# Multi-query attention on one core: 32-row score tiles, the mask inside the maximum, and TensorE's other work as one piece per head between the second and third fill

## The chip, the cores and the metric

One Trainium2 chip, one of its cores. The metric is the device time of one execution in microseconds, as the median of several runs. TensorE multiplies matrices, VectorE, ScalarE and GpSimd (POOL) do elementwise work and reductions, SyncE (SP) issues the DMAs. SBUF is the on-chip memory of 128 partitions; PSUM, where TensorE writes, has eight banks of 128 x 512 f32. The engines run their own instruction queues in order and wait for each other by semaphores.

## The reference, cut to what matters

The whole computation is a multi-query attention, a transformer of six layers with local attention, and normalisations around both. The change touches the first alone (here with B, S = 8, 512):

```python
D_MODEL, NUM_HEADS, HEAD_DIM = 128, 16, 8
Q = (x @ Wq + bq).reshape(B, S, H, Dh).transpose(0, 2, 1, 3)
K = x @ Wk + bk                      # one set of keys for all 16 heads
V = x @ Wv + bv
A = jnp.einsum('bhqd,bkd->bhqk', Q, K)
causal = jnp.tril(jnp.ones((S, S), dtype=bool))
A = jnp.where(causal, A, -jnp.inf)
P = jax.nn.softmax(A / np.sqrt(Dh).astype(np.float32), axis=-1)
O = jnp.einsum('bhqk,bkd->bhqd', P, V)
return O.transpose(0, 2, 1, 3).reshape(B, S, H * Dh) @ Wo + bo
```

## The kernel before

`mqa_stage` runs the attention for 8 batches of 16 heads, 128 heads in a pipeline that `steps()` counts as n, with batch b = n // 16 and head h = n % 16. Each engine has its own loop over the same steps, and what it does in a step is written out by hand with `if h == ...`. Four heads are a group (`PER_GROUP`); `i` is the head's place in it.

Each head is scored twice. `scores` computes query-by-key scores, six heads ahead (`AHEAD`), only to find each query's largest score. They go into two PSUM banks, `score[0]` and `score[1]`, in fills: query tile 3 (512 keys), then tile 2 (384) together with tile 0 (128), then tile 1 (256), which two neighbouring heads share, so five fills a pair (`PAIR_FILLS`). Each fill waits until the maximum of the fill two before it is taken (`at_least(pe, s_max, fill - 1)`). VectorE's `maxima` reduces them. GpSimd's `negated_maxima` writes the negated maximum, split into two f32r parts, into two further columns of the queries. `turn_with_max` transposes these queries, and `scoresT` computes key-by-query scores with the maximum already subtracted, into three banks `scoreT[0..2]` (512, 384 + 128 and 256 columns), from which ScalarE's `exps` writes the probabilities. GpSimd's `causal` zeroes their upper triangles. `weighted_values` multiplies them with the values and a column of ones, in 128*32 tiles, one column tile a head of the group. After a transpose VectorE's `weighted` divides by the sums.

A head has 8 values a slot of 32 rows (`SLOTS`): high parts, low parts, the high parts again, and the maximum's two. Four heads lie under each other in the 128 rows of `qT0` and `qT1`. All matmuls of scores use all 128 rows, so the keys of head place i must be zero in the other 96: GpSimd's `spread_keys` makes four copies `kT[:, i, :]` of `k_flat`, each multiplied by a 0/1 column `own_rows`. The causal mask of the diagonal blocks is added by a further bf16 matmul of the identity and `mask_qk`, on top of each fill.

On TensorE, a step first issues `scoresT(n, k)` and `scores(n + AHEAD, k)` in turn for k = 0, 1, 2, and then what else is due: values and their transposes, the input's transposes and projection (`turn_xn`, `project`), keys and queries (`turn_keys`, `turn_queries`), and for the batch before `turn_attn`, `project_out` and `turn_y`. One bank, `near`, takes the results of most of them, another, `out_bank`, the last three; `take` waits until the bank's last user is done. ScalarE's loop does the three exponentials of a step and then the copies out of these banks. `hi_parts` and `lo_parts` (ScalarE, VectorE) split the projection. VectorE takes the maxima first, then `weighted`, `lo_parts` and the statistics of the normalisations; GpSimd normalises.

The rest of the kernel (`layers_stage`, `output_stage`) is untouched. Its line numbers occur in rows of the trace: L1256 to L1258 are projections with 512 columns, L1284 are scores in 64*32 tiles.

## Time and profile before

| | us |
|---|---|
| median of 3 runs (lowest, highest) | 3549.22 (3547.38, 3552.28) |
| the profiled execution | 3546.17 |
| its span in the trace | 3544.4 |

Busy time over the span: TensorE matmuls 3327.0 us (94%), VectorE 2958.5 (83%), ScalarE 2699.2 (76%), GpSimd 2594.4 (73%). The multi-query stage is about the first eighth of the span; the layers are the rest. The shares over the whole span therefore say little about this stage, and its own stretches have to be read. How a line of the groups is read: line of the kernel, engine, operation, output <- inputs, shapes, count, then busy time and mean ns of one, then idle time of the engine before them and who ended it. A line in order of time has its start, its duration, the engine, the line, the count that it merges, and in brackets the idle time before it with its releaser. Durations of matmuls include their way through the array, so their starts tell the pace better than their ends.

### The profile page before, as it was taken

The page shows a single profiled execution, that of the slowest core. Times are in us where ns is not written, and L with a number is a line of the kernel's source. Part 1 is how long each engine was busy: PE and PEld are TensorE (multiplying, and loading weights), DVE is VectorE, ACT ScalarE, POOL GpSimd, SP SyncE. Part 2 cuts the span into 40 slices and gives each one's busy share as a digit, 9 for nine tenths or more (in the row PEclk, how much of TensorE's full clock was granted, in tenths as well). Part 3 has the DMA queues.
Part 4 walks back from the last instruction along what each step waited for, and adds up shares of the span by engine and source line. Part 5 has one row for each costly group of instructions (what it writes and reads, how often), then busy time and mean ns, then how long its engine had stood idle before and what let it go on. Part 6 is the DMA issues. An engine that isn't in the chain of part 4 may idle for free. (4 is left out here: it accounts for less than half of the span.)

```text
span 3544.4 us, 158585 instructions
## 1 busy us (share of the span) xinstructions
PE 3327.0 (94%) x66425; PEld 2792.0 (79%) x66426; DVE 2958.5 (83%) x4037; ACT 2699.2 (76%) x4132; POOL 2594.4 (73%) x3334
## 2 busy tenths in 40 slices
PE   7999759999999999999999999999999999999995
PEld 5666547888788888788888888888888888888874
DVE  6666568888888888988888888889888889888874
ACT  4666547888788888788888788887788888888873
POOL 4676567777777777777777777777777777777772
PEclk9999879999999999999999999999999999999997
DMA  2000013222223222223222232222232222222222
GB/s 59 4 7 7 10 48 92 67 65 70 71 71 90 68 65 69 72 72 89 70 67 64 77 96 65 65 71 59 77 96 70 65 67 66 70 72 71 67 59 66
DMA packets 161748, 228.22 MB, mean 64 GB/s; under 512 B 42264, under 2 KB 60640, under 8 KB 161504
## 3 DMA queue, kind: packets, MB, share of 16 engines
q1 hardware_dynamic: 161632, 226.85, 23.8%
q8 instruction: 51, 0.84, 0.1%
q14 instruction: 65, 0.53, 0.0%
HBM read 21.00 MB, written 4.19 MB: 7 GB/s over the span
## 5 line engine op out<-in xcount | busy, mean ns | idle before, releaser
L1170 POOL TENSOR_TENSOR by_cos<-by_cos,by_sin 128x1024 f32<-128x1024 f32 x384 | 910.7, 2382 | 12.5 <-DVE by_sin L1524 12.5
L1176 POOL TENSOR_TENSOR by_cos<-by_cos,norms 128x1024 f32<-128x1024 f32 x384 | 733.8, 1911 | 13.0
L1522 DVE TENSOR_TENSOR by_cos<-proj,turns 128x1024 f32<-128x1024 f32 x384 | 470.0, 1224 | 177.9 <-ACT squares L1412 152.7
L1256 PE MATMUL proj<-qkv_hi,xs_hib 128*128 128x512 f32 x1152 | 512.5, 445 | 48.3 <-DVE by_sin L1524 39.3
L1524 DVE TENSOR_TENSOR by_sin<-proj,turns 128x1024 f32<-128x1024 f32 x384 | 466.1, 1214 | 0.0
L1528 DVE TENSOR_REDUCE sumsb<-squares 128x16 f32<-128x1024 f32 x384 | 464.4, 1209 | 1.5 <-DVE w_lo L1591 1.5
L1258 PE MATMUL proj<-qkv_hi,xs_lob 128*128 128x512 f32 x1152 | 458.1, 398 | 0.0
L1257 PE MATMUL proj<-qkv_lo,xs_hib 128*128 128x512 f32 x1152 | 457.9, 397 | 0.0
L1412 ACT ACTIVATE squares<-proj 128x1024 f32<-128x1024 f32 x384 | 392.6, 1022 | 82.7 <-PE proj L1258 81.9
L1265 PE MATMUL ring<-ident,by_cos 128*128 128x128 f32 x3072 | 385.4, 273 | 8.2 <-DVE xT L1625 4.9
L1392 ACT ACTIVATE vb<-proj 128x1024 f32<-128x1024 f32 x192 | 195.0, 1016 | 257.0 <-DMA v_win<-vb 225.5
L1265 PEld LDWEIGHTS ring<-ident,by_cos 128*128 128x128 f32 x3072 | 349.9, 141 | 35.2 <-issue 7.5
L1319 PE MATMUL ring<-attnT,wo 128*128 128x256 f32 x1536 | 347.2, 379 | 1.5 <-ACT attnT L1392 1.5
L1184 POOL TENSOR_TENSOR xs_lob<-xsb,xs_hib 128x128 fp32r<-128x128 f32 x192 | 88.3, 460 | 349.8 <-ACT xs_hib L1392 349.8
L1319 PEld LDWEIGHTS ring<-attnT,wo 128*128 128x128 f32 x1536 | 291.3, 190 | 44.8 <-ACT attnT L1392 2.0
L1256 PEld LDWEIGHTS proj<-qkv_hi,xs_hib 128*128 128x128 f32 x1152 | 219.0, 190 | 108.6 <-DVE by_sin L1524 61.0
L1305 PEld LDWEIGHTS ring<-v_win,pTb 64*32 64x32 f32 x24576 | 254.7, 105 | 56.4 <-issue 56.4
L1284 PEld LDWEIGHTS score<-kTb,qTb 64*32 64x32 f32 x24576 | 255.0, 105 | 54.4 <-issue 42.1
L1305 PE MATMUL ring<-v_win,pTb 64*32 64x64 f32 x24576 | 286.6, 226 | 7.5 <-issue 7.5
L1284 PE MATMUL score<-kTb,qTb 64*32 64x64 f32 x24576 | 286.5, 226 | 5.4 <-issue 4.8
L1392 ACT ACTIVATE kTb<-ring 128x1024 f32<-128x1024 f32 x192 | 197.7, 1030 | 101.5 <-PE ring L1265 101.0
L1258 PEld LDWEIGHTS proj<-qkv_hi,xs_lob 128*128 128x128 f32 x1152 | 218.6, 190 | 52.4
(196 smaller groups left out, 7985.6 us busy)
## 6 DMA issues: line engine op xcount, KB each, us to landing
v_win<-vb SPq DMA_DIRECT2D x1152, 128.0 KB, 2.3
v_win<-vb SPq DMA_DIRECT2D x768, 64.0 KB, 2.0
in_qkv<-L_ffn_Wqkv SPq DMA_DIRECT2D x12, 768.0 KB
wo<-L_ffn_Wo SPq DMA_DIRECT2D x6, 512.0 KB, 4.1
x_tok<-L_attn_x SPq DMA_DIRECT2D x8, 256.0 KB, 4.2
residual<-x_tok SPq DMA_DIRECT2D x8, 256.0 KB, 2.0
o_x<-residual SPq DMA_DIRECT2D x1, 2048.0 KB, 8.4
out<-o_x SPq DMA_DIRECT2D x8, 256.0 KB, 2.2
```

What stands on the lines that cost most here:

```text
L1170: nc.gpsimd.tensor_tensor(both, both, by_sin[:, j, :], ALU.add).then_inc(e[f"{w_}_added"].sem, 1)
L1176: nc.gpsimd.tensor_tensor(heads, heads, inverse, ALU.mult).then_inc(e[f"{w_}_ready"].sem, 1)
L1256: nc.tensor.matmul(out, xs_hi[:, tile], qkv_hi[:, cols], start=True, stop=False)
L1257: nc.tensor.matmul(out, xs_hi[:, tile], qkv_lo[:, cols], start=False, stop=False)
L1258: last = nc.tensor.matmul(out, xs_lo[:, tile], qkv_hi[:, cols], start=False, stop=True)
L1265: last = nc.tensor.transpose(out[:, i * P:(i + 1) * P], by_cos[:, t % 2, j, i * P:(i + 1) * P], ident[:, :])
L1284: last = nc.tensor.matmul(score[queries, at:at + KEYS], qT[rows, t % 2, i, queries], keys, start=False, stop=True, skip_group_check=True)
L1305: last = nc.tensor.matmul(out[queries, at:at + DH], pT[rows, i, queries], v_win[rows, t % 2, n, i, :], start=True, stop=True)
L1319: last = nc.tensor.matmul(out[:, 0:HS], wo[:, i, :], attnT[:, i, :], start=(i == 0), stop=(i == PAIRS - 1))
L1522: nc.vector.tensor_tensor(of_heads(by_cos[:, t % 2, j, :]), heads, table(0), ALU.mult)
L1524: nc.vector.tensor_tensor(swapped, heads, table(1), ALU.mult).then_inc(e[f"{w_}_rotated"].sem, 1)
L1528: nc.vector.tensor_reduce(sums[:, t % 2, j, :, 0], squares[:, :].rearrange("p (h d) -> p h d", d=DH), AX.X, ALU.add).then_inc(e[f"{w_}_sum ...
```

## The change

- `scores` and `scoresT` use the 32 rows of the head's own slot alone (`rows`), so `spread_keys`, `k_flat` and `own_rows` go; `kT` is one copy, which ScalarE writes out of `near`.
- The mask matmuls go. `maxima` is now one `tensor_tensor_reduce` each: scores plus an f32 mask row from SBUF, with the maximum as accumulator, its elementwise result into a scratch tile `masked`.
- Tile 1 has a fill of its own for each head: three fills a head (`FILLS`), six for a pair.
- All other TensorE work moves into `between(n, b, h)`, which stands between the second and the third fill of each step, with a new timetable; the values are split in two halves (i = 1 and 2). ScalarE has the same `between` ahead of its third exponential.
- VectorE takes the first two maxima of a step, then statistics, then the third, then `weighted` and `lo_parts`. Output normalisation and y come later by several heads, the input's normalisation earlier by one batch.
- The pipeline runs six steps longer.

```diff
-PAIR_FILLS = 5
+FILLS = 3
+QUERIES_AT = (8, 11, 12, 15)
+SUM_STATISTICS_AT = (6, 8, 9, 10)
-FIRST_STEP, LAST_STEP = -MQA_H, HEADS + 2 * MQA_H
+FIRST_STEP, LAST_STEP = -MQA_H, HEADS + 2 * MQA_H + 6
...
-    first = PAIR_FILLS * (m // 2)
-    return ((3, first), (2, first + 1), (1, first + 2)) if m % 2 == 0 else ((3, first + 3), (2, first + 4))
+    return (3, FILLS * m), (2, FILLS * m + 1), (1, FILLS * m + 2)
...
-        k_flat, own_rows = sb("a_k_flat", [P, S]), sb("a_own_rows", [P, PER_GROUP])
-        kT = [sb(f"a_kT{p}", [P, PER_GROUP, S], F32R) for p in range(2)]
+        kT = [sb(f"a_kT{p}", [P, S], F32R) for p in range(2)]
...
             def scores(m, qt, fill):
+                rows = slice(SLOTS * i, SLOTS * i + SLOTS)
                 out, keys = score[fill % 2], kT[b % 2]
                 at_least(pe, s_max, fill - 1)
-                queries = lambda k: qT0[:, g, k * P:(k + 1) * P]
+                queries = lambda k: qT0[rows, g, k * P:(k + 1) * P]
                 if qt == 3:
-                    if i % 2 == 0:
+                    if i == 0:
                         pe.wait_ge(q_done, GROUPS * b + g + 1)
-                        pe.wait_ge(keys_done, PER_GROUP * b + i + 2)
-                    nc.tensor.matmul(out[:, :], queries(3), keys[:, i, :], start=True, stop=True,
-                                     skip_group_check=True)
-                    masked, mask = out[:, 3 * P:4 * P], mask_qk[:, 0, :]
+                        pe.wait_ge(keys_done, b + 1)
+                    last = nc.tensor.matmul(out[:, :], queries(3), keys[rows, :], start=True, stop=True)
...
-                nc.tensor.matmul(masked, ident_bf[:, :], mask, start=False, stop=True,
-                                 skip_group_check=True).then_inc(s_full, 1)
+                    last = nc.tensor.matmul(out[:, 0:2 * P], queries(1), keys[rows, 0:2 * P], start=True, stop=True)
+                last.then_inc(s_full, 1)
...
+                    last = nc.tensor.matmul(scoreT[k][:, at:at + width], kT[b % 2][rows, kt * P:(kt + 1) * P],
+                                            qT1[rows, g, kt * P:S], start=True, stop=True)
...
+            def between(n, b, h):
+
+                group, i = n // PER_GROUP - 1, h % PER_GROUP
+                new, old, oldest = b + 1, b - 1, b - 3
+                if 0 <= group < B * GROUPS:
+                    if i in (1, 2):
+                        weighted_values(group, (0, 1) if i == 1 else (2, 3))
+                    elif i == 3:
+                        turn_values(group)
+                if i == 2 and 0 <= group + 2 < B * GROUPS:
+                    turn_with_max(group + 2)
+                if batch_of(new):
+                    if h == 0:
+                        turn_xn(new)
+                    elif h in (3, 4):
+                        project(new, h - 3)
+                    elif h == 7:
+                        turn_keys(new)
+                    elif h in QUERIES_AT:
+                        turn_queries(new, QUERIES_AT.index(h))
+                if batch_of(old):
+                    if h == 8:
+                        turn_attn(old)
+                    elif h == 12:
+                        project_out(old)
+                if batch_of(oldest) and h == 4:
+                    turn_y(oldest)
...
                 for k in range(3):
+                    if k == 2:
+                        between(n, b, h)
                     if 0 <= n < HEADS:
                         scoresT(n, k)
                     if k < len(ahead):
                         scores(n + AHEAD, *ahead[k])
...
             def maxima(m, qt, fill):
                 dve.wait_ge(s_full, fill + 1)
+                at_least(dve, s_max, fill - FILLS + 1)
+
+                def largest(qt, at):
+                    n = (qt + 1) * P
+                    place = slice((fill % FILLS) * S + at, (fill % FILLS) * S + at + n)
+                    return nc.vector.tensor_tensor_reduce(
+                        out=masked[:, place], in0=score[fill % 2][:, at:at + n], in1=mask_qk[:, 4 * P - n:4 * P], scale=1.0,
+                        scalar=LOWEST, op0=ALU.add, op1=ALU.max, accum_out=row_max[:, qt, h:h + 1])
...
-                for fill in fills(n + AHEAD):
+                new, old, older = b + 1, b - 1, b - 2
+                ahead = fills(n + AHEAD)
+                for fill in ahead[0:2]:
+                    maxima(n + AHEAD, *fill)
...
+                for fill in ahead[2:]:
                     maxima(n + AHEAD, *fill)
                 group = n // PER_GROUP - 1
                 if h % PER_GROUP == 3 and 0 <= group < B * GROUPS:
                     weighted(group)
-                if batch_of(new) and h in (4, 5):
-                    lo_parts(new, h - 4)
+                if batch_of(new) and h in (3, 4):
+                    lo_parts(new, h - 3)
```

## Rows read from the trace of the kernel before

**Rows 1.** One line of the kernel, the exponentials: durations, first and last start.
```profile
L545 ACT ACTIVATE a_probs<-a_scoreT x384: 383/594/674, 39.5 to 415.8; 128x512 f32<-128x512 f32 x128, 128x256 f32<-128x256 f32 x64
```

**Rows 2.** Busy time by stretch: length, busy (instructions) by engine, clock, DMA.
```profile
200.00:300.00 100.00, 94.63 (x773) 67.91 (x771) 67.49 (x176) 68.18 (x154) 70.10 (x129) 1.00 0.02 7
```

**Rows 3.** In order of time: the stage's last copy.
```profile
436.67 0.60 ACT L537 ACTIVATE xT<-a_out_bank 128x512 f32<-128x512 f32 x1 [6.94 <-PE a_out_bank L370]
```

**Rows 4.** In order of time, TensorE matmuls: an even and an odd head.
```profile
225.28 0.47 PE L411 MATMUL a_scoreT<-a_qT,a_kT 128*128 128x512 f32 x1
225.59 0.39 PE L383 MATMUL a_score<-a_kT,a_qT 128*128 128x512 f32 x1
225.82 0.23 PE L399 MATMUL a_score<-a_mask_qk,ident_bf 128*128 128x128 bf16 x1
...
227.30 0.60 PE L370 MATMUL a_near<-ident,a_qa 128*128 128x128 f32 x4
227.74 0.60 PE L370 MATMUL a_values<-ident,a_pvb 128*128 128x128 f32 x4
228.09 0.48 PE L411 MATMUL a_scoreT<-a_qT,a_kT 128*128 128x512 f32 x1
...
229.77 0.39 PE L383 MATMUL a_score<-a_kT,a_qT 128*128 128x512 f32 x1
```

**Rows 5.** The same view: values, the output projection, half an input projection.
```profile
208.45 0.48 PE L480 MATMUL a_out_bank<-a_bias,a_ones_r 128*128 128x512 f32 x1
...
209.57 0.48 PE L411 MATMUL a_scoreT<-a_qT,a_kT 128*128 128x512 f32 x1
...
233.60 2.36 PE L422 MATMUL a_values<-a_probs,a_va 128*32 128x512 f32 x32
235.89 0.50 PE L411 MATMUL a_scoreT<-a_qT,a_kT 128*128 128x512 f32 x1
...
243.72 0.38 PE L452 MATMUL a_near<-a_bias,a_ones_r 128*128 128x288 f32 x1
...
244.33 0.49 PE L411 MATMUL a_scoreT<-a_qT,a_kT 128*128 128x512 f32 x1
```

**Rows 6.** The same view in the layers: full tiles, then 64*32 tiles.
```profile
1522.09 0.40 PE L1258 MATMUL proj<-qkv_hi,xs_lob 128*128 128x512 f32 x1
1522.42 1.48 PE L1284 MATMUL score<-kTb,qTb 64*32 64x64 f32 x128
```

**Rows 7.** In order of time, TensorE and VectorE: maxima between fills.
```profile
36.89 0.28 PE L399 MATMUL a_score<-a_mask_qk,ident_bf 128*128 128x256 bf16 x1
...
37.21 0.56 DVE L742 TENSOR_REDUCE a_row_max<-a_score 128x1 f32<-128x384 f32 x1
...
37.68 0.28 DVE L743 TENSOR_REDUCE a_row_max<-a_score 128x1 f32<-128x128 f32 x1
37.88 0.68 DVE L745 TENSOR_REDUCE a_row_max<-a_score 128x2 f32<-128x512 f32 x1
...
38.02 0.50 PE L383 MATMUL a_score<-a_kT,a_qT 128*128 128x512 f32 x1
```

**Rows 8.** Groups by line and shape, the first 600 us: keys, a two-operand addition.
```profile
L281 POOL TENSOR_SCALAR a_kT<-a_k_flat,a_own_rows 128x512 fp32r<-128x512 f32 x32 | 49.6, 1562 | 2.1 <-ACT a_k_flat L537 2.1
...
L1522 DVE TENSOR_TENSOR by_cos<-proj,turns 128x1024 f32<-128x1024 f32 x19 | 23.3, 1224 | 33.4 <-ACT squares L1412 26.2 <-PE ring L1265 7.0
```

**Rows 9.** In order of time, VectorE: half of the low parts, `weighted`.
```profile
17.02 0.42 DVE L731 TENSOR_TENSOR a_qa<-a_near,a_qa 128x256 fp32r<-128x256 f32 x1 [2.40 <-ACT a_va L537]
...
205.80 0.25 DVE L752 RECIPROCAL a_recipb<-a_values 128x16 f32<-128x16 f32 x1
...
206.19 0.29 DVE L757 TENSOR_TENSOR a_attnb<-a_values,a_recipb 128x128 f32<-128x128 f32 x1
```

**Rows 10.** The same view at the start: first fill, first maximum.
```profile
22.80 0.77 PE L383 MATMUL a_score<-a_kT,a_qT 128*128 128x512 f32 x1 [0.33 <-POOL a_kT L281]
...
27.86 0.68 DVE L740 TENSOR_REDUCE a_row_max<-a_score 128x1 f32<-128x512 f32 x1
```

More of the change, by code:

```diff
@@ L166, in mqa_stage @@
         no_max = sem("no_max")
[L167 removed]
+        k_full, keys_done = sem("k_full"), sem("keys")
         q_full, q_done = sem("q_full"), sem("q")
@@ L309, in _ @@
                     negated_maxima((n + AHEAD) // PER_GROUP)
-                new, old, older = b + 1, b - 1, b - 2
+                next_, new, older = b + 2, b + 1, b - 2
                 if n == FIRST_STEP:
@@ L399, in scores @@
-                nc.tensor.matmul(masked, ident_bf[:, :], mask, start=False, stop=True,
-                                 skip_group_check=True).then_inc(s_full, 1)
+                    nc.tensor.matmul(out[:, 0:3 * P], queries(2), keys[rows, 0:3 * P], start=True, stop=True)
+                    last = nc.tensor.matmul(out[:, 3 * P:4 * P], queries(0), keys[rows, 0:P], start=True, stop=True)
+                else:
+                    last = nc.tensor.matmul(out[:, 0:2 * P], queries(1), keys[rows, 0:2 * P], start=True, stop=True)
@@ L407, in scoresT, with weighted_values @@
                     pe.wait_ge(t2_done, GROUPS * b + g + 1)
-                at = 0
+                at, rows = 0, slice(SLOTS * i, SLOTS * i + SLOTS)
                 for kt in PROB_BANKS[k]:
                     width = S - kt * P
-                    last = nc.tensor.matmul(scoreT[k][:, at:at + width], kT[b % 2][:, i, kt * P:(kt + 1) * P],
-                                            qT1[:, g, kt * P:S], start=True, stop=True)
+                    last = nc.tensor.matmul(scoreT[k][:, at:at + width], kT[b % 2][rows, kt * P:(kt + 1) * P],
+                                            qT1[rows, g, kt * P:S], start=True, stop=True)
                     at += width
                 last.then_inc(st_full, 1)
-            def weighted_values(group):
-                pe.wait_ge(causal_done, PER_GROUP * (group + 1))
-                at_least(pe, attn_done, group)
-                for kt in range(TILES):
+            def weighted_values(group, tiles):
+                if 0 in tiles:
+                    pe.wait_ge(causal_done, PER_GROUP * (group + 1))
+                    at_least(pe, attn_done, group)
+                for kt in tiles:
                     for i in range(PER_GROUP):
@@ L424, in weighted_values @@
                                                 start=(kt == 0), stop=(kt == TILES - 1))
-                last.then_inc(pv_full, 1)
+                if TILES - 1 in tiles:
+                    last.then_inc(pv_full, 1)
             def turn_values(group):
@@ L460, in turn_keys @@
                 pe.wait_ge(lo_done, 2 * b + 2)
-                take("near", (k_flat_done, b + 1))
+                take("near", (keys_done, b + 1))
                 turned(near, [ka[:, t, :, :].bitcast(F32).rearrange("p r s -> p (r s)") for t in range(TILES)], k_full)
@@ L603, in _, with between @@
             nc.scalar.activation(c["exp_warm"][:, :], c["minus_half"][:, 0:1], ACT.Exp)
[L604 to L606 removed]
+            def between(n, b, h):
                 group = n // PER_GROUP - 1
[L608 to L612 removed]
+                new, old, oldest = b + 1, b - 1, b - 3
+                if h % PER_GROUP == 2:
+                    if 0 <= group < B * GROUPS:
+                        values_group(group)
+                    if 0 <= group + 2 < B * GROUPS:
+                        turned_with_max(group + 2)
                 if batch_of(new):
[L614 removed]
+                    if h == 0:
                         turned_input(new)
[L616 to L617 removed]
+                    elif h in (3, 4):
+                        hi_parts(new, h - 3)
                     elif h == 7:
                         keys_turned(new)
[L620 to L623 removed]
+                    elif h in QUERIES_AT:
+                        queries_turned(new, QUERIES_AT.index(h))
                 if batch_of(old):
[L625 removed]
+                    if h == 8:
                         attn_turned(old)
[L627 removed]
+                    elif h == 12:
                         output(old)
[L629 to L630 removed]
+                if batch_of(oldest) and h == 4:
+                    output_turned(oldest)
+            for n, b, h in steps():
+                for k in range(3):
+                    if k == 2:
+                        between(n, b, h)
+                    if 0 <= n < HEADS:
+                        exps(n, k)
         @block.vector
```

188 lines of the change are left out of this document (55 added, 133 removed).

## The prediction

> **What bounds the kernel now.** I read the views from the outside in. First the span of the exponentials and the busy time by stretch [rows 1, 2]: the multi-query stage starts its exponentials, three a head for 128 heads, between 39.5 and 415.8 us; the last start is the last head's third, so 376.3 us hold about 127.6 heads, 2.95 us each, and the stage's last copy ends at 437.3 [rows 3]. The diff touches nothing behind that, so the question is what 2.95 us becomes. In 200 to 300 us TensorE is busy 95% of the time; VectorE, ScalarE and GpSimd stand at 67 to 70%, about 2.0 us a head. The granted clock there is 1.00, the 2.4 GHz level. So TensorE sets the pace, and I went on to its order of time in one pair of heads [rows 4].
>
> In rows 4 an even head's scores and transposed scores run from 225.28 to 227.30 = 2.02 us. The odd one starts at 228.09; the next head's first fill starts at 229.77 and lies 0.31 behind the transposed scores before it (as 225.59 does behind 225.28), so the odd head took 229.46 - 228.09 = 1.37. The mean is 1.70 us. The reader is to see that starts follow each other by columns: 512 columns take 0.23 (225.59 to 225.82).
>
> The rest of TensorE's work is the "pieces" [rows 5]. Two groups of four transposes take 228.09 - 227.30 = 0.79, so 0.40 a group. The weighted values of a group of four heads take 235.89 - 233.60 = 2.29, the output projection 209.57 - 208.45 = 1.12, half of an input projection 244.33 - 243.72 = 0.61. Per four heads come one set of values and three transposes; per batch of 16 heads four more transposes (input, keys, attention, y), two halves and one output projection. Per head: 2.29/4 + 3 x 0.40/4 + (4 x 0.40 + 2 x 0.61 + 1.12)/16 = 0.57 + 0.30 + 0.25 = 1.12. 1.70 + 1.12 = 2.82 of the 2.95; the rest is waits for maxima.
>
> **Part by part: what TensorE loses and gains.** The two and a half mask matmuls of a head go, and the shared fill of two heads becomes one fill of 256 columns a head. Scores and transposed scores then are 1280 columns each, 2560 x 0.23/512 = 1.15 us; I add 0.10 for the two 128-column matmuls, which are short beside their weight loads: 1.25 against 1.70. That is 0.45 us a head saved if nothing else changes.
>
> Against it stands the change of tile shape. Every one of the 16 pieces now stands between 32-row matmuls, so each head enters another shape and comes back. The trace of before has no 32-row tile. The nearest rows are the layers' 64*32 tiles [rows 6]: the 512-column matmul in front starts at 1522.09, and the tiled ones at 1522.42, 0.33 instead of 0.23. I take 0.10 for each change of shape, both ways, with bounds 0 and 0.20: 0.20 a head. The values split in two pay two more, 0.20 per four heads, 0.05 a head. The trace so bears out that a change costs something. The Trainium skill ("TensorEngine Tiling (Array Packing)", Key Properties) states it as a rule against this change: changing the tiling mode drains the engine, while another tile of the same mode does not. It gives no price.
>
> TensorE's own work then is 1.25 + 1.12 + 0.05 + 0.20 = 2.62 us a head, if matmuls of different row groups don't overlap.
>
> **The reductions on VectorE.** Four reductions a head instead of three and a half, over the same 1280 elements. Spacing [rows 7]: 37.21 to 37.68 for 384 elements is 0.47, 37.68 to 37.88 for 128 is 0.20, so 1.05 ns an element and 0.065 fixed. 1280 elements in four instructions are 1.35 + 0.26 = 1.61 us. The new instruction adds the mask from SBUF. A two-operand one with PSUM and SBUF inputs takes 1224 ns for 1024 elements [rows 8], about the same slope plus start, so the adding is free. What the accumulator's write-out costs no row shows: bounds are 0 and 0.20 each (a 128-element instruction). I take 0.07, the fixed part of one more instruction, since it moves a single column. That is 1.87 a head. Weighted values cost 205.80 to 206.48 = 0.68 per four heads [rows 9], and the statistics and low parts lift the sum to about 2.3, under TensorE's. The Trainium skill ("VectorE: DVE Perf Modes", Two Vector instructions with no wait between them) says that an operation that also writes out its accumulator is two instructions; no row here shows it.
>
> **The wait that the change adds.** There are two score banks and three fills a head, so fill k waits for the maximum of fill k-2. With the piece between the second and the third fill, the second fill of a head waits for the third maximum of the head before, which waits for the third fill, which stands in TensorE's queue behind the whole piece. TensorE's first fill and two transposed scores can run beside it, the piece can't. From the start of a second fill to the next:
> - its 512 columns 0.23, change of shape 0.10, the piece, change back 0.10
> - transposed scores of 256 columns ahead of the third fill: 0.12 alone, 0 if side by side; I take 0.06
> - the third fill, 256 columns, lasts 0.28, then 0.04 until VectorE starts (36.89 + 0.28 = 37.17, start 37.21) [rows 7]
> - maximum of 256 elements: 0.28 + 128 x 1.05 ns = 0.41, and 0.07 for the accumulator
> - back to TensorE 0.06 (37.68 + 0.28 = 37.96, the next fill starts at 38.02).
>
> Sum without the piece 1.35 us. The mean piece is 1.12 + 0.05 = 1.17, so 2.52.
>
> Some heads take longer, because VectorE's `weighted` comes after the third maximum and the next two maxima behind it. After it VectorE needs 0.68 + (0.60 + 0.47 + 0.20) + 3 x 0.07 = 2.16 until it can take a third maximum again; that fill is there after 0.87 + piece. The pieces at heads 0, 4, 8 and 12 are 0.40, 1.01, 0.80 and 1.52, so VectorE is late by 0.9, 0.3, 0.5 and 0. At head 4 another wait decides: `project` of the second half needs `lo_done` of the first, which VectorE makes after `weighted`, 0.68 + at least 0.42 [rows 9] after the third maximum; TensorE is there 0.39 after it. About 0.8 us, and behind it in TensorE's queue stand the y transposes, the transposed scores and the third fill. Together 0.9 + 0.8 + 0.5 = 2.2 us per batch, 0.14 a head. The two bounds (TensorE's 2.62, the ring of waits 2.52 + 0.14) lie side by side; I take 2.70, which leaves 0.04 for their meeting.
>
> **Off the path.** Spreading the keys goes from GpSimd, 32 instructions of 1562 ns, 0.39 us a head [rows 8]; GpSimd stands at 70%, so it buys nothing in the steady part. At the start TensorE's first fill waited 0.33 us for the spread keys and began at 22.80, but the first maximum began only at 27.86 [rows 10], behind the statistics in VectorE's queue; I take nothing. ScalarE has the same exponentials and copies, one key copy for one. Its copies now stand ahead of the third exponential, at most two of 0.60 us [rows 3], with 2.70 - 2.0 = 0.7 us of slack a head. No DMA moves except that the residual stores of a batch start later; the last one's chain (projection, two normalisations, y) is the same instructions in the same order, so the 21 us behind the last exponential stay. If ScalarE's cover is gone, it costs up to 0.6 us on one head in four, 0.15 a head.
>
> **Sum.** Heads with scores still ahead are 122 of 128. (2.95 - 2.70) x 122 = 30.5 us. The profiled run took 3546.17 (span 3544.4, 1.8 around it); 3546.2 - 30.5 = 3515.7. The median of the runs is 3.1 above the profiled one, so 3519.
>
> **Bounds.** Everything at its low end (no cost of shape, no accumulator, transposed scores side by side): 2.70 - 0.20 - 0.05 - 0.07 - 0.06 = 2.32, 77 us, 3472. Everything at its high end (0.20 for each change, 0.20 for the accumulator, 0.12 for the transposed scores): 2.70 + 0.20 + 0.05 + 0.13 + 0.06 = 3.14, 23 us slower, 3572.
>
> **Rivals.**
> 1. Row groups run side by side, and switching is nearly free: 2.35 to 2.55 a head, bound by VectorE (2.3) and the piece; 3475 to 3500. For it: 128 instructions of 64 columns in 64*32 tiles last 1.48 us [rows 6], 12 ns each, where 64 columns at 2.4 GHz alone are 27 ns, so tiles do overlap; but those tiles differ in columns too. The heads n and n+6 lie two row groups apart. Against it: the ring of waits has only one such pair in it. The Trainium skill ("TensorE: Matmul & The Clock Gate", Part 3) says that a single 32-row matmul takes as long as a full one and that the gain is concurrency, measured at 3.07 times for four tiles.
> 2. The ring eats the gain: shape changes near 0.20 each, 2.87 to 3.05 a head; 3540 to 3561. For it: a set of values in 128*32 tiles is entered and left by such changes too. Against it: the 0.10 of rows 6.
> 3. Slower, by VectorE: the fused reduction costs more than a plain one. VectorE's sum is 1.61 + 0.42 + 4a; it passes 2.95 when a, the surcharge of one instruction, passes 0.23 us. At 0.35, or two cycles an element (+1.33 a head), VectorE needs 3.4: 122 x 0.45 = 55 us, 3604. Against it: the two-operand row of rows 8.
> 4. Slower, by the clock: with a quarter of the rows at work and a wait a head, the granted clock falls to the 1.2 GHz level in part of the stage. TensorE's 2.62 doubles; for half of the stage that is 2.3 x 61 = 140 us, 3660. Against it: 1.00 in rows 2, and the longest new wait in the sum is 0.8 us.
>
> **How the numbers follow.** Forecast (3500 to 3535) 0.47; rival 1 0.18; rival 2 0.20; rival 3 0.10; rival 4 0.03; 0.02 for a stall in start or end. The range 3478 to 3566 leaves out rivals 3 and 4 and the ends of the bounds. A measurement tells 0.2%, 7 us, which is 0.06 us a head. Faster by more: 0.47 + 0.18 + 0.03 of rival 2 = 0.68; within: 0.09 of rival 2 and 0.01 = 0.10; slower: 0.08 + 0.10 + 0.03 + 0.01 = 0.22.
>
> **What would show it.** In the profile after: the exponentials' last start near 385 us; a second fill that starts 0.06 behind the third maximum of the head before; starts around a piece 0.10 wider than columns; 256-element reductions about 0.41 long, with or without a second instruction; a TensorE idle of 0.8 us before `project` at head 4. VectorE busy above 90% would make rival 3 right; a granted clock under 1.00 in 100 to 300 us rival 4. The prediction is wrong where the ring isn't what TensorE waits for, or the new instruction's price is far from 0.07.

## The result and the profile after

The kernel after takes 3588.85 us (median of 7 runs, 3566.93 to 3592.98) against 3549.22 (3547.38 to 3555.35): the ratio is 1.0099, 95% interval 1.0076 to 1.0121, so 1% slower. The prediction was 3519, faster. The profiled execution took 3592.98, its span 3591.0.

The first view is the exponentials' line, as in [rows 1] (durations, first and last start), and the busy time by stretch, as in [rows 2]: length, busy (instructions) for TensorE, its weight loads, VectorE, ScalarE, GpSimd, then the granted clock, the DMA share and GB/s.

```profile
L528 ACT ACTIVATE a_probs<-a_scoreT x384: 377/597/672, 42.5 to 463.6; 128x512 f32<-128x512 f32 x128, 128x256 f32<-128x256 f32 x64
```

```profile
100.00:200.00 100.00, 94.06 (x604) 57.69 (x605) 59.08 (x273) 57.67 (x133) 41.48 (x94) 0.74 0.01 4
200.00:300.00 100.00, 92.12 (x658) 56.58 (x660) 65.98 (x308) 61.94 (x142) 56.84 (x116) 0.85 0.02 7
300.00:400.00 100.00, 92.55 (x652) 58.39 (x640) 64.85 (x306) 61.76 (x143) 52.28 (x110) 0.82 0.02 6
```

The exponentials hold 421.1 us instead of 376.3, 44.8 more; the span grew by 46.6. All of the loss is in the attention. A head takes 421.1/127.6 = 3.30 us. TensorE's busy share is that of before (92 to 94% against 94.63), but the granted clock is 0.74 to 0.85 where [rows 2] had 1.00. With two levels, 2.4 and 1.2 GHz, a mean clock c means that 2(1 - c) of the stretch ran at the lower: 52, 30 and 36 us, 118 of these 300.

The clock column reads 1.00 ahead of the first change on record, which comes at 77.1 us. The matmuls show that the clock was low up to there. TensorE in order of time, one head of the start and two heads later on (a start, a duration, the tile and shape; in brackets the idle time before it):

```profile
65.58 0.57 PE L379 MATMUL a_score<-a_kT,a_qT 32*128 32x256 f32 x1
65.59 0.79 PE L391 MATMUL a_scoreT<-a_qT,a_kT 32*128 32x512 f32 x1
65.59 0.79 PE L374 MATMUL a_score<-a_kT,a_qT 32*128 32x512 f32 x1
...
66.72 0.68 PE L376 MATMUL a_score<-a_kT,a_qT 32*128 32x384 f32 x1
...
70.47 0.68 PE L376 MATMUL a_score<-a_kT,a_qT 32*128 32x384 f32 x1
```

```profile
246.62 0.38 PE L391 MATMUL a_scoreT<-a_qT,a_kT 32*128 32x256 f32 x1
...
246.62 0.38 PE L379 MATMUL a_score<-a_kT,a_qT 32*128 32x256 f32 x1
...
246.63 0.49 PE L391 MATMUL a_scoreT<-a_qT,a_kT 32*128 32x512 f32 x1
...
246.63 0.50 PE L374 MATMUL a_score<-a_kT,a_qT 32*128 32x512 f32 x1
...
247.56 0.44 PE L376 MATMUL a_score<-a_kT,a_qT 32*128 32x384 f32 x1 [0.20 <-DVE a_row_max L727]
...
247.84 0.22 PE L377 MATMUL a_score<-a_kT,a_qT 32*128 32x128 f32 x1
...
247.99 0.66 PE L360 MATMUL a_values<-ident,a_pvb 128*128 128x128 f32 x4
...
248.48 0.60 PE L360 MATMUL a_near<-ident,a_qa 128*128 128x128 f32 x4
...
249.01 0.38 PE L379 MATMUL a_score<-a_kT,a_qT 32*128 32x256 f32 x1
...
249.46 0.42 DVE L727 CUSTOM_DVE_ANT_0 a_masked<-a_score,a_mask_qk 128x256 f32<-128x256 f32 x1 [0.38 <-PE a_score L379]
...
249.81 0.08 DVE L727 DVE_READ_ACCUMULATOR2_ANT a_row_max<- 128x1 f32 x1
...
249.95 0.44 PE L376 MATMUL a_score<-a_kT,a_qT 32*128 32x384 f32 x1 [0.20 <-DVE a_row_max L727]
```

A matmul of 512 columns lasts 0.79 us in the first block and 0.50 in the second: the first is at 1.2 GHz, the second at 2.4. A head at the start takes 3.75 us (66.72 to 70.47), the same kind of head later 2.39 (247.56 to 249.95). Between the first and the last exponential 203 of the 421 us are at the half clock, 34.6 of them before 77.1, the rest mostly in stretches of 17 to 27 us, about one a batch (118.1 to 142.0 is the first).

What does that cost? The kernel rows128 below, the same but for the rows of the scores, takes 2.66 us a head with no lowered clock. Against it the heads of the kernel after that run at the full clock take 0.09 more (the same places in the batch, from the exponentials' starts), so a head at the full clock is about 2.75, and 127.6 of them are 350 us. That leaves 71 of the 421 us for the clock, 0.35 us lost for each us at the half clock. Two batches of 16 heads inside the kernel after agree: the fourth takes 48.2 us with 6.8 at the half clock, the fifth 54.4 with 23.9, a difference of 6.2 us for 17.1. The span of the exponentials is 421.1 - 127.6 x 2.70 = 77 us over the prediction: 71 of these are the clock's.

### The profile page after: what moved, and what is told of

It is laid out like the page before. It is cut to its first block and busy times, and to the rows that moved or that the text cites. A ratio compares the mean times of both kernels' runs of the same rounds, so it can differ in the third digit from the quotient of the medians.

```text
span 3591.0 us, 158808 instructions
## 1 busy us (share of the span) xinstructions
PE 3366.3 (94%) x66105; PEld 2775.8 (77%) x66106; DVE 2965.7 (83%) x4608; ACT 2691.8 (75%) x4132; POOL 2549.4 (71%) x3302
## 5 line engine op out<-in xcount | busy, mean ns | idle before, releaser
L1256 PEld LDWEIGHTS ring<-ident,by_cos 128*128 128x128 f32 x3072 | 350.2, 141 | 34.6 <-issue 7.5
L727 DVE CUSTOM_DVE_ANT_0 a_masked<-a_score,a_mask_qk 128x512 f32<-128x512 f32 (+3 forms) x512 | 229.5, 487 | 143.4 <-PE a_score L379 130.9
```

Of the source, the lines that this page charges most:

```text
L1256: last = nc.tensor.transpose(out[:, i * P:(i + 1) * P], by_cos[:, t % 2, j, i * P:(i + 1) * P], ident[:, :])
```

## The experiments

Every kernel is timed against the kernel before; the medians of that lay between 3544.52 and 3549.45 us. "Half clock, 100 to 400" is the sum of 2(1 - c) over three stretches of 100 us, which a reader can repeat from the windows; the next column is the whole time between first and last exponential, with the start by the durations of matmuls; "last" is the last exponential's start.

| kernel | rows of scores | median us | ratio (95%) | last | half clock, 100 to 400 | half clock, all |
|---|---|---|---|---|---|---|
| before | 128 | 3549.22 | 1 | 415.8 | 0 | 3 |
| after | 32 | 3588.85 | 1.0099 (1.0076, 1.0121) | 463.6 | 118 | 203 |
| rows128 | 128 | 3516.12 | 0.9915 (0.9898, 0.9931) | 379.7 | 0 | 0 |
| rows64 | 64 | 3544.52 | 0.9995 (0.9985, 1.0005) | 404.2 | 16 | 35 |
| fill128 | 32, and filler on 128 | 3582.88 | 1.0109 (1.0092, 1.0125) | 452.8 | 40 | 79 |
| fill32 | 32, and filler on 32 | 3606.35 | 1.0170 (1.0153, 1.0187) | 474.9 | 92 | 154 |
| late_pieces | 32 | 3622.11 | 1.0208 (1.0191, 1.0225) | 502.5 | 126 | 256 |
| thin128 | 128, few columns | 3513.18 | 0.9908 (0.9889, 0.9928) | 372.7 | 0 | 3 |
| before_fused | 128 | 3559.49 | 1.0038 (1.0024, 1.0052) | 424.1 | 0 | 7 |
| rows128_attn7 | 128 | 3514.32 | 0.9911 (0.9894, 0.9927) | 375.9 | 0 | 0 |
| before_rows32 | 32 for most | 3612.96 | 1.0178 (1.0161, 1.0195) | 478.9 | 78 | 124 |
| scores32 | 32 and 128 | 3665.28 | 1.0353 (1.0317, 1.0389) | 521.1 | 52 | 97 |
| after_attn7 | 32 | 3563.45 | 1.0029 (1.0015, 1.0044) | 442.6 | 88 | 165 |

(The 3, 3 and 7 us of before, thin128 and before_fused lie ahead of 58 us; from there to the last exponential the clock of the kernels with all scores on 128 rows is 1.00. What lies behind the last exponential isn't counted, so the windows of rows128, thin128 and rows128_attn7, which end at 373 to 380 us, give more than the table.) The times themselves are medians of 2 to 10 runs; the clock columns are of the one profiled run.

**rows128: is it the rows?** The kernel after with scores on all 128 rows and the keys spread by GpSimd as before; timetable, fills and fused maxima stay.

```diff
-                out, keys = score[fill % 2], kT[b % 2]
+                out, keys = score[fill % 2], kT[b % 2][:, i, :]
...
-                queries = lambda k: qT0[rows, g, k * P:(k + 1) * P]
+                queries = lambda k: qT0[:, g, k * P:(k + 1) * P]
...
-                    last = nc.tensor.matmul(out[:, :], queries(3), keys[rows, :], start=True, stop=True)
+                    last = nc.tensor.matmul(out[:, :], queries(3), keys[:, :], start=True, stop=True)
...
-                    last = nc.tensor.matmul(scoreT[k][:, at:at + width], kT[b % 2][rows, kt * P:(kt + 1) * P],
-                                            qT1[rows, g, kt * P:S], start=True, stop=True)
+                    last = nc.tensor.matmul(scoreT[k][:, at:at + width], kT[b % 2][:, i, kt * P:(kt + 1) * P],
+                                            qT1[:, g, kt * P:S], start=True, stop=True)
```

> The changed kernel with scores and transposed scores back on all 128 rows (four zero-padded copies of the keys, spread by GpSimd); schedule and fused maximum stay. If the clock fell because the score matmuls use a quarter of the rows, or because they overlap and leave TensorE waiting, the granted clock is 1.00 from 80 to 400 us, and a head takes 2.6 to 2.75 us by the ring of waits: about 3510 to 3525, 0.99 of before. If the clock fell because of the new timetable (pieces of transposes alone between waits), half-clock stretches remain and the time stays above 3560.

Measured: 3516.12, 0.9% faster than before, (379.7 - 40.9)/127.6 = 2.66 us a head, and no lowered clock. In the third to seventh batch, 14 of the 16 places have heads at the full clock in both kernels; by their medians they take 37.5 us here and 38.7 in the kernel after, 0.09 us a head more on 32 rows: at equal clocks the 32-row tiles gain nothing, and cost a little. Its exponentials, its windows, and TensorE around a piece:

```profile
L538 ACT ACTIVATE a_probs<-a_scoreT x384: 372/599/667, 40.9 to 379.7; 128x512 f32<-128x512 f32 x128, 128x256 f32<-128x256 f32 x64
```

```profile
200.00:300.00 100.00, 96.62 (x780) 72.78 (x778) 79.19 (x365) 73.75 (x168) 80.38 (x146) 1.00 0.02 7
```

```profile
242.31 0.22 PE L387 MATMUL a_score<-a_kT,a_qT 128*128 128x128 f32 x1
242.37 0.60 PE L371 MATMUL a_values<-ident,a_pvb 128*128 128x128 f32 x4
242.81 0.60 PE L371 MATMUL a_near<-ident,a_qa 128*128 128x128 f32 x4
243.17 0.36 PE L401 MATMUL a_scoreT<-a_qT,a_kT 128*128 128x256 f32 x1
```

In 96 of the 128 rows the keys are zeros here, so the products are, and the clock still stays at 2.4 GHz. The queries in these rows are those of the other heads and not zero; rows with zeros on both sides weren't tried. The same lines price the change of shape. A 128-column matmul ahead of a piece takes 0.06 here (242.31 to 242.37) and 0.15 in the kernel after (247.84 to 247.99); the last transposes take 0.36 to the next matmul here and 0.53 there (248.48 to 249.01). That is 0.09 into the piece and 0.17 out of it.

**late_pieces: is it the timetable?** The pieces stand behind the third fill again, where before had the rest of the work; `turn_attn` is at head 7.

```diff
                 for k in range(3):
-                    if k == 2:
-                        between(n, b, h)
...
+                between(n, b, h)
```

> The changed kernel with 32-row tiles, but each piece behind the third fill instead of ahead of it, on TensorE and ScalarE alike; the transposes of the attention one head earlier, since the order would not run otherwise. The wait from third fill to second fill then has no piece in it. At full clock a head takes 2.4 to 2.5 us, by TensorE's own work and VectorE's. If rows decide the clock it still falls to half in stretches, with more than 80 us at half, and the time is 3550 to 3590. If the waits in the ring decide it, TensorE waits less and the clock stays: 3490 to 3500.

Measured: 3622.11, above both expected ranges, with 256 us at the half clock, and at the full clock about 3.0 us a head. Taking the wait for the maxima away from the piece did not restore the clock. The expected 2.4 to 2.5 us a head was wrong as well: with the pieces behind all three fills the fills come in one bunch, and each head's third one waits for the maximum, at the full clock too:

```profile
228.76 0.33 PE L376 MATMUL a_score<-a_kT,a_qT 32*128 32x384 f32 x1
...
228.94 0.22 PE L377 MATMUL a_score<-a_kT,a_qT 32*128 32x128 f32 x1
...
229.75 0.38 PE L379 MATMUL a_score<-a_kT,a_qT 32*128 32x256 f32 x1 [0.42 <-DVE a_row_max L725]
```

**rows64: a dose between.** Tiles of 64 rows, two spread copies of the keys; the diff is that of rows128 with `rows = slice(64 * (i // 2), 64 * (i // 2) + 64)`.

> Scores and transposed scores in 64-row tiles, two zero-padded copies of the keys, else as the changed kernel. Between 32 rows (203 us of 421 at the half clock, 3589) and 128 rows (none, 3516). Tiles of heads n and n+6 still lie side by side and each piece still changes the shape. If the rows decide the clock, the half-clock time lies between the two, 30 to 150 us, and the kernel at 3520 to 3565. If any overlap or change of shape brings the clock down, it is as bad as with 32 rows, 3575 to 3600. If the clock holds throughout, a head takes about 2.70 us and the kernel 3520.

Measured: 3544.52, the same as before; 35 us at the half clock. Rows 32, 64, 128 give 203, 35 and 0 us. The changes of shape around a piece are as many here as on 32 rows, so they alone don't make the 203. They cost time at the full clock too: a batch without any half clock takes 45.3 us (the fourth), against 43.7 in rows128.

**fill128 and fill32: columns or rows?** Two more matmuls of 256 columns a head of ones by ones, into the bank that the third transposed scores then overwrite; on 128 rows in one kernel, on 32 in the other.

```diff
                 at, rows = 0, slice(SLOTS * i, SLOTS * i + SLOTS)
+                if k == 2 and True:
+                    for _ in range(2):
+                        nc.tensor.matmul(scoreT[2][:, 0:256].rearrange("p (t n) -> p t n", t=2), ones_r[:, :],
+                                         ones_r[:, :].unsqueeze(1).broadcast_to([128, 2, P]),
+                                         start=True, stop=True)
                 for kt in PROB_BANKS[k]:
```

The edit is in `scoresT`; fill32 has `ones_r[rows, :]` and `[32, 2, P]` in it.

> The changed kernel plus two matmuls of 256 columns on all 128 rows ahead of each head's third transposed scores, into the bank that these overwrite. They add 0.22 to 0.25 us a head to the ring at full clock: 2.72 + 0.23 = 2.95. If full rows hold the clock, it stays at 1.00 and the time is that of before, 3540 to 3560. If the clock falls for another reason, 3610 or more.

> The same two added matmuls of 256 columns, in the same place, on 32 rows (the row group of the head) instead of 128. The same columns and the same wait. If rows decide the clock, it falls as in the changed kernel or more, and the time is 3600 to 3640. If the time in which TensorE streams decides, the clock rises as with 128 rows and the time is 3540 to 3560.

Measured: the same columns on 128 rows leave 79 us at the half clock, on 32 rows 154; without them there are 203. Full rows do more than thin ones, and thin ones do something. Neither fits its expectations in full: fill128, at 3582.88, lies between its two, as full rows for part of the columns don't hold the clock all the time, and on fill32 the half clock shrank where "as in the changed kernel or more" was expected. (Head for head both cost more than they give back: a full-clock head takes 3.05 and 2.98 us.)

**thin128: waits and columns with full rows.** rows128 with only 128 columns a score matmul, 512 instead of 1280 a head. The maxima read the columns that are there repeatedly, so they take as long as before, but they aren't the maxima of all keys.

```diff
-                    last = nc.tensor.matmul(out[:, :], queries(3), keys[:, :], start=True, stop=True)
+                    last = nc.tensor.matmul(out[:, 0:P], queries(3), keys[:, 0:P], start=True, stop=True)
```

> The 128-row variant with only the first 128 keys of each score fill computed (512 columns a head instead of 1280); VectorE reads those columns repeatedly, so that its time stays, and the maxima are not the true ones. TensorE streams 1792 columns a head on all rows for scores and transposed scores, about 0.8 us, as little as the overlapped 32-row version's 0.7, and waits about as long. If rows decide the clock, it stays at 1.00 between 80 and 370 us. If the time in which TensorE streams decides, half-clock stretches of 100 us or more come back. At full clock 2.5 to 2.65 us a head.

Measured: 3513.18, and the clock at 1.00 from 44 us on:

```profile
100.00:200.00 100.00, 93.74 (x784) 69.64 (x783) 76.82 (x363) 74.54 (x170) 77.57 (x139) 1.00 0.02 7
200.00:300.00 100.00, 94.56 (x800) 68.80 (x800) 79.48 (x372) 74.02 (x168) 81.56 (x153) 1.00 0.02 7
```

So few columns don't bring the clock down: 1792 score columns in a head of 2.60 us are 690 a us, against 2560/2.75 = 930 in the kernel after at the full clock. TensorE's busy share needs more care. The 94.06 of the kernel after in 100 to 200 us holds 52 us of half-clock time, in which every matmul lasts longer. At the full clock, between its start and its first fall, the kernel after is busy for 89%; before_fused, the next kernel, is busy for 91% and stays at 1.00; and before_rows32, below, is busy for 99% in a stretch that ends with a fall:

```profile
77.10:118.10 41.00, 36.52 (x309) 22.77 (x305) 29.02 (x129) 29.60 (x69) 19.30 (x47) 1.00 0.00 1
```

```profile
100.00:200.00 100.00, 90.65 (x686) 67.87 (x685) 67.02 (x321) 65.83 (x149) 65.42 (x123) 1.00 0.02 7
```

```profile
124.30:158.40 34.10, 33.62 (x249) 20.97 (x248) 22.92 (x57) 23.57 (x52) 19.66 (x36) 1.00 0.00 1
```

The Trainium skill ("TensorE: Matmul & The Clock Gate", Part 1, What's actually happening) says that the gate is set by how busy TensorE has been. By that rule the 99% stretch should hold the clock better than the 91% one; the traces show that the rows in use count too.

**before_fused: the fused maximum alone.** The kernel before, with three fills a head, and the mask in the maximum; 128 rows, old timetable.

```diff
-    first = PAIR_FILLS * (m // 2)
-    return ((3, first), (2, first + 1), (1, first + 2)) if m % 2 == 0 else ((3, first + 3), (2, first + 4))
+    return (3, FILLS * m), (2, FILLS * m + 1), (1, FILLS * m + 2)
...
-                nc.tensor.matmul(masked, ident_bf[:, :], mask, start=False, stop=True,
-                                 skip_group_check=True).then_inc(s_full, 1)
+                last.then_inc(s_full, 1)
```

> One part of the change alone: the kernel before, with its own timetable and 128-row tiles, but three fills a head, no mask matmuls and the mask inside the maximum. TensorE's own work falls from 2.82 to about 2.5 us a head. With the pieces behind the third fill, the fused maxima of VectorE (about 2.0 us a head) run beside them. If the timetable matters little, it is as fast as the 128-row variant of the change, 3510 to 3520. If the spread is what lets the fills and maxima overlap, it is at 3525 to 3545.

Measured: 3559.49, 0.4% slower than before and above both expected ranges, 3.00 us a head, with the clock at 1.00. The waits in 100 to 360 us (total, times, longest):

```profile
DVE a_masked L729 <- PE a_score L382: 56.8, 51, 2.6
...
PEld a_score L387 <- DVE a_row_max L729: 37.1, 84, 1.0
```

Three fills a head through two banks turn into waits of TensorE for VectorE, while VectorE waits for TensorE during the pieces. With the new timetable, a piece between the fills, the work that the mask matmuls free does become time: rows128 is 43 us faster than this one.

**rows128_attn7 and after_attn7: the wait that the prediction missed.** VectorE's `weighted` writes into the buffer that `turn_attn` reads. At head 7 it has to wait for `turn_attn` at head 8, and the third fill of head 8 then waits for a maximum. The edit, in TensorE's and in ScalarE's loop:

```diff
-                    if h == 8:
+                    if h == 7:
                         turn_attn(old)
```

> The 128-row variant with the attention's transposes one head earlier (7 instead of 8), on TensorE and ScalarE. VectorE's `weighted` at head 7 then no longer waits for a piece of head 8: 8.2 us in 100 to 360 us, 1.4 a batch. If that wait was on the path, about 1 us a batch goes, 3508 to 3512; if VectorE had the time, no change, 3516.

Measured on 128 rows: 3514.32 against 3516.12; the wait is gone, the 1.8 us are within the uncertainty. On 32 rows the wait stands close to the clock's falls. In the kernel after, VectorE and TensorE in order of time:

```profile
116.58 0.29 DVE L744 TENSOR_TENSOR a_attnb<-a_values,a_recipb 128x128 f32<-128x128 f32 x1 [1.52 <-PE a_out_bank L360]
...
117.85 0.38 PE L379 MATMUL a_score<-a_kT,a_qT 32*128 32x256 f32 x1 [1.07 <-DVE a_row_max L727]
```

> The kernel after, on 32 rows, with the attention's transposes one head earlier (head 7 instead of head 8, in TensorE's and ScalarE's loops). In the kernel after VectorE's weighted waits for them at head 7, and the third fill of head 8 then waits 0.55 to 1.07 us for a maximum, every 16 heads (117.85, 172.26, 226.32, 274.81, 328.90, 380.65 us); the clock falls at 118.1, 169.3, 227.3, 275.1, 329.7, 380.9, so within about 1 us behind that wait in five of six. Theory (rows in use alone): the falls stay, somewhere around heads 7 to 10, where the pieces are transposes alone: 150 to 210 us at the half clock and 3575 to 3595 us. Rival (the wait on few rows is what starts each fall; on 128 rows, where the clock stays at 1.00, the same wait is 0.94 us long and harmless): the wait goes and most falls with it, under 100 us at the half clock and 3530 to 3560 us.

Measured: 3563.45 (3551.83 to 3575.00; the profiled one is the 3575.00), 165 us at the half clock. The time lies between the two expectations. The falls no longer come at head 8 of each batch: there are short ones of 3.4 us (at 141.4, 165.3, 189.2, 332.6 and 370.1 us), longer ones at 295.0 and 394.0 (20.5 and 17.1 us) and a long one, 233.6 to 277.9. So the wait isn't the cause, since the falls stay without it, and on 128 rows its 0.94 us did nothing to the clock; but on few rows taking it away gave 25 us, of which its own length is 4.6 (1.07 + 0.55 + 4 x 0.75); the rest fits the clock, since 203 - 165 = 38 us less at 0.35 are 13, and the two profiled runs differ by 18.0. The time of the kernels on few rows differs from run to run with the falls (the fastest run of the kernel after, 3566.93, has a mean clock of 0.971, the others 0.961 to 0.965), so one profile shows a sample of them.

**before_rows32: the rows alone, on the old timetable.**

```diff
-                queries = lambda k: qT0[:, g, k * P:(k + 1) * P]
+                own = lambda j: slice(SLOTS * j, SLOTS * j + SLOTS)
+                queries = lambda k: qT0[own(i), g, k * P:(k + 1) * P]
...
-                    nc.tensor.matmul(out[:, :], queries(3), keys[:, i, :], start=True, stop=True,
+                    nc.tensor.matmul(out[:, :], queries(3), keys[own(i), i, :], start=True, stop=True,
...
-                                            qT1[:, g, kt * P:S], start=True, stop=True)
+                                            qT1[own, g, kt * P:S], start=True, stop=True)
```

> The kernel before, its timetable, its fills and its mask matmuls kept, but the tile-3, tile-2 and tile-0 scores and all transposed scores use the head's own 32 rows alone; the shared fill of tile 1 stays on 128 rows. The output is the same. Theory (rows in use set the clock; 32 rows in the kernel after gave 203 us at the half clock, 64 gave 35, 128 none): here 512 + 384 + 128 + 1280 = 2304 of 2560 score columns a head go down to 32 rows, but half a tile-1 fill and the mask matmuls stay whole, so full rows are a good third of the columns. I expect a granted clock under 1.00 in 100 to 400 us, 50 to 150 us at the half clock, and 3600 to 3650 us, as changes of shape (0.10 to 0.17 each, some six a head) come on top. Rival (the new timetable lets the clock fall, not the rows): clock 1.00 in 100 to 400 us as in the kernel before, and only the changes of shape are paid: about 3570 to 3600 us.

Measured: 3612.96, inside the theory's range, and the clock falls without the new timetable:

```profile
100.00:200.00 100.00, 99.03 (x680) 58.22 (x680) 59.39 (x147) 60.78 (x134) 57.38 (x107) 0.88 0.01 4
200.00:300.00 100.00, 99.10 (x678) 56.96 (x681) 58.76 (x155) 59.92 (x131) 59.52 (x111) 0.87 0.02 6
```

TensorE is busy 99% of the time here, more than in any other kernel, and is at the half clock for a quarter of it. Busy time includes what the changes of shape cost, so the columns are the better check: 2560 of the scores and 512 of the masks in a head of 3.41 us are 900 a us, against the 690 of thin128, with the same other work in a longer head. The clock falls on more score columns a us, of which most are on 32 rows.

**scores32: is it the tiles that run side by side?** The diff is against rows128: transposed scores on 128 rows, scores on 32, so that no two neighbours share a shape.

```diff
-                out, keys = score[fill % 2], kT[b % 2][:, i, :]
+                out, keys = score[fill % 2], kT[b % 2][SLOTS * i:SLOTS * i + SLOTS, i, :]
...
-                queries = lambda k: qT0[:, g, k * P:(k + 1) * P]
+                queries = lambda k: qT0[SLOTS * i:SLOTS * i + SLOTS, g, k * P:(k + 1) * P]
```

> The kernel after with the spread keys, as in rows128, but only the transposed scores use all 128 rows; the scores stay on 32 rows. The output is the same. Theory (rows in use times columns): half of the score columns are back on all rows, in every head, so between rows128 (0 us at the half clock) and the kernel after (203): like rows64, under 60 us at the half clock. Every fill now changes shape, six changes a head, and nothing runs side by side, so 2.75 to 3.1 us a head at the full clock and 3530 to 3575 us. Rival (side-by-side tiles of different row groups lower the clock, not the rows): nothing of two shapes runs side by side here, so 0 us at the half clock, as in rows128. A result of over 100 us at the half clock would speak against both.

Measured: 3665.28, the slowest. Nothing runs side by side, and still 97 us are at the half clock, so the overlap isn't needed for the falls. That is above the 60 us expected, and the head takes 3.56 at the full clock instead of 2.75 to 3.1, because a change of shape at every matmul costs twice what I had taken:

```profile
246.18 0.50 PE L401 MATMUL a_scoreT<-a_qT,a_kT 128*128 128x512 f32 x1
246.60 0.49 PE L384 MATMUL a_score<-a_kT,a_qT 32*128 32x512 f32 x1
247.02 0.50 PE L401 MATMUL a_scoreT<-a_qT,a_kT 128*128 128x384 f32 x2
```

512 columns take 0.42 to the next start instead of 0.23.

What the runs leave open: how the rows, the columns and the changes of shape weigh against each other (203, 154, 97 and 79 us fit more than one rule). The change to small tiles always brought changes of shape with it; rows64 and after show that these alone don't set the size, but no run has small tiles without them. Nor was it tried whether 32-row tiles of one row group, never side by side, would behave otherwise, or rows with zeros on both sides. And where in a batch the clock falls isn't explained: in the kernel after it is mostly at heads 8 and 9, behind pieces of transposes alone, but rows128 has the same pieces there and stays at 1.00.

## Why the prediction was wrong, by its own steps

- **The step that failed** is the dismissal of rival 4. It was named with its mechanism, a quarter of the rows at work, and given 0.03, "against it: 1.00 in rows 2, and the longest new wait in the sum is 0.8 us". Neither speaks against it: rows 2 shows a kernel with all rows at work, and the waits were taken as what lowers the clock. thin128 waits and stays at 1.00; before_rows32 hardly waits and falls. No row of before has 32-row tiles for a whole stage, so the trace had no evidence against it, and the chance should have been like that of any unseen resource. The size was off the other way: the rival doubled TensorE's 2.62 for half the stage and came to 3660. (Its 2.3 a head is the step up from the 2.95 of before, but it was added to the 3519 of the forecast; from 2.70 the same assumption gives 155 us and 3674.) Measured are 0.35 us lost for each us at the half clock, 71 us for 203. In the heads shown above the same work goes from 2.39 to 3.75, not to twice as much: the waits for VectorE shrink.
- **The sum at the full clock was nearly right**: 2.70 predicted, about 2.75 in the kernel after, 6 of the 77 us. That is in part luck, since its terms erred both ways. In the head shown above the ring takes 2.39 where the terms give 1.35 + 0.80 = 2.15: the second fill's two matmuls 0.28 + 0.06 instead of 0.23, the piece 0.85 instead of 0.80, the changes of shape 0.26 instead of 0.20, from the third fill's start to its maximum 0.45 instead of 0.38, the maximum to the next fill 0.49 (0.35 + 0.08 + 0.06) instead of 0.54. What gives most of it back on other heads is in part VectorE, below, and a shorter wait ahead of `project`, 0.55 instead of 0.8; the rest I haven't separated.
- **The order of the ring** was right: the second fill starts 0.06 behind the end of the accumulator's read (249.81 + 0.08 to 249.95), as [rows 7] gave for the plain maximum.
- **VectorE** was over-priced. Its groups in 0 to 500 us (busy, mean ns; idle time before):

```profile
L727 DVE CUSTOM_DVE_ANT_0 a_masked<-a_score,a_mask_qk 128x512 f32<-128x512 f32 x128 | 87.6, 685 | 5.3 <-PE a_score L374 4.5 <-issue 0.2 <-PE a_score L377 0.2
...
L727 DVE CUSTOM_DVE_ANT_0 a_masked<-a_score,a_mask_qk 128x256 f32<-128x256 f32 x128 | 54.1, 422 | 131.0 <-PE a_score L379 130.9
L727 DVE DVE_READ_ACCUMULATOR2_ANT a_row_max<- 128x1 f32 x512 | 42.2, 82 | 0.0
...
L744 DVE TENSOR_TENSOR a_attnb<-a_values,a_recipb 128x128 f32<-128x128 f32 x32 | 9.3, 291 | 11.9 <-PE a_out_bank L360 11.0
```

  The fused maximum runs at the plain one's pace (685 ns for 512 elements, 0.68 in [rows 7]). The Trainium skill ("VectorE: DVE Perf Modes", Two Vector instructions with no wait between them) has an accumulator's write-out as a second instruction, and the trace agrees, 82 ns each. But the next maximum starts beside it:

```profile
117.72 0.08 DVE L727 DVE_READ_ACCUMULATOR2_ANT a_row_max<- 128x1 f32 x1
117.72 0.55 DVE L727 CUSTOM_DVE_ANT_0 a_masked<-a_score,a_mask_qk 128x384 f32<-128x384 f32 x1
118.19 0.08 DVE L727 DVE_READ_ACCUMULATOR2_ANT a_row_max<- 128x1 f32 x1
118.19 0.28 DVE L727 CUSTOM_DVE_ANT_0 a_masked<-a_score,a_mask_qk 128x128 f32<-128x128 f32 x1
```

  0.47 from the 384-element maximum to the next, the 0.47 of [rows 7] exactly: a is 0 to 0.02, not 0.07. The price is paid once a head, where TensorE waits for the read. Rival 3 fell. The idle 131.0 us ahead of the 256-element maxima are the ring, seen from VectorE.
- **Side by side**, rival 1's premise, was true: in the block above four matmuls start at 246.62, 246.62, 246.63 and 246.63. They are of four row groups, since they belong to the heads n, n+6, n+1 and n+7. It didn't bring the rival's time, because the ring, from one second fill to the next, has only one such pair in it, as the text said, and because the clock fell.
- **A wait was missed**: `weighted` at head 7 against `turn_attn` at head 8, the 11.0 us of L744 above and 0.55 to 1.07 us of TensorE a batch. The prediction followed the moved steps through TensorE's queue and not through the buffer that two of them share.
- **The start** was taken at nothing. The first exponential starts 3.0 us later (42.5 for 39.5), and the clock rises at 77.1 us where in the kernel before the matmuls of 512 columns last 0.50 (the 38.02 of [rows 7]) before the 39.5 of the first exponential. This is in the 203 us.

## What to carry to other kernels

A row-tiled matmul can give the same result for the same columns and still cost the clock: padded with zeros to all 128 rows the same change is 0.9% faster than before, on 32 rows 1% slower. Ask of every change that shrinks the tiles whether anything in the trace shows that shape at work for a whole stage; where nothing does, the low clock deserves a real chance, not 0.03. And a piece of other work between two fills that wait for each other's bank hides that wait, which a bunch of fills and a bunch of pieces don't (rows128 against before_fused, where the whole timetable differs, and on 32 rows the kernel after against late_pieces, about 2.75 and 3.0 us a head at the full clock, where nearly only the place of the pieces does).

## What the runs showed of the hardware that was not expected

- The granted clock follows the rows in use: 203, 35 and 0 us at the half clock on 32, 64 and 128 rows, with TensorE's busy share in 100 to 300 us at 92 to 97% in all three. Rows in which only the keys are zero count as use (rows128). A kernel on 32 rows for most scores is busy for 99% and at the half clock for a quarter of 100 to 400 us.
- Entering full tiles from 32-row tiles costs 0.09 us, leaving them 0.17, and 0.19 at every matmul where each changes the shape.
- Matmuls of four 32-row groups start within 0.01 us of each other (246.62 to 246.63), and so do pairs of 64-row tiles (244.84 and 244.85 in rows64).
- The read of VectorE's accumulator, 82 ns, lies beside the next reduction, and is only paid by who waits for it.
